# Edge-weighted mean layer of a graph network: per-step sums accumulated in PSUM instead of added by VectorE

## The reference, cut to what matters

```python
msg = h[src] * e                     # e: 100000 x 64 edge attributes
summed = segment_sum(msg, dst, 3125)
cnt = segment_sum(ones, dst, 3125)
h_total = concatenate([h, summed / maximum(cnt, 1)], axis=1)
return h_total @ W.T + b
```

## Time and profile before

| | us |
|---|---|
| Median of 3 runs | 5527.91 |
| Lowest and highest of them | 5525.43, 5542.02 |
| Span of the profiled execution, first to last instruction | 5821.8 |
| of it, the stage of the change (first attribute load to last add) | 2793.1 to 3980.2 |
| of it, the fourth layer's gathers | 4076.3 to 5382.3 |

### The profile page before, as it was taken

The page is one execution under the profiler, slowest core; times in us unless marked ns, Lnnn a source line. Parts: engine busy times, 40 slices in busy tenths (PEclk is TensorE's granted clock), DMA queues, the critical chain, the costliest instruction groups (busy, mean ns, idle before and its releaser), DMA issues. The chain is left out here.

```text
span 5821.8 us, 59032 instructions
## 1 busy us (share of the span) xinstructions
PE 3339.7 (57%) x14332; PEld 2165.0 (37%) x14332; DVE 3534.5 (61%) x6569; ACT 2187.4 (38%) x3989; POOL 2214.4 (38%) x2086
## 2 busy tenths in 40 slices
PE   5666679999999999789034332333000443433565
PEld 3555534444444444456032332333000443333452
DVE  6999989999999999310134332333211664545676
ACT  4999967878788887200000000000000111111210
POOL 0000023333333333000666777772777056666200
PEclk8999989999999999899556555555555555555556
DMA  2555544444444443787321422212111012111011
GB/s 74 163 162 162 162 131 114 119 111 111 119 109 116 116 115 97 155 187 157 57 45 38 92 47 43 50 34 22 35 28 33 9 33 36 31 36 30 5 36 35
DMA packets 546254, 474.35 MB, mean 81 GB/s; under 512 B 185774, under 2 KB 439737, under 8 KB 545086
## 3 DMA queue, kind: packets, MB, share of 16 engines
q1 hardware_dynamic: 493723, 416.13, 28.5%
q0 software_dynamic: 52288, 55.34, 5.9%
HBM read 351.39 MB, written 119.84 MB: 81 GB/s over the span
## 5 line engine op out<-in xcount | busy, mean ns | idle before, releaser
L815 PE MATMUL l_sum_ps<-arena,sums 125*65 125x500 f32 (+1 forms) x2600 | 1144.6, 578 | 9.9 <-ACT arena L776 4.8
L1740 POOL DMA_INDIRECT l_rows<-table,tile_src x782 | 768.9, 983 | 521.1 <-issue 232.6
L1143 POOL DMA_INDIRECT l_rows<-hidden_rows,tile_src x782 | 794.9, 1017 | 341.8 <-issue 231.5
L694 POOL COPY arena<-arena 125x750 f32<-125x750 f32 (+1 forms) x400 | 538.9, 1351 | 894.6 <-PE l_count_ps L804 864.9
L760 ACT ACTIVATE arena<-arena,far_left 125x750 f32<-125x750 f32 (+1 forms) x800 | 713.3, 939 | 285.7 <-DVE arena L713 285.7
L713 DVE SCALAR_TENSOR_TENSOR arena<-arena,far_past 125x750 f32<-125x750 f32 (+1 forms) x800 | 807.1, 1055 | 16.1 <-DMA arena<-score_rows 16.1
L1204 PE MATMUL l_sum_ps<-l_rows,l_hot 128*125 x1612 | 360.1, 414 | 768.6 <-issue 651.9
L724 DVE SCALAR_TENSOR_TENSOR arena<-arena,l_count_ps 125x750 f32<-125x750 f32 (+1 forms) x800 | 739.4, 970 | 100.5 <-ACT arena L765 52.0
L1934 PE MATMUL l_sum_ps<-l_rows,l_hot 128*128 x1962 | 483.6, 424 | 439.3 <-issue 268.9
L1170 DVE TENSOR_TENSOR sums<-sums,l_sum_ps 125x64 f32 x806 | 178.6, 222 | 777.9 <-DMA arena<-counts 485.6
L1204 PEld LDWEIGHTS l_sum_ps<-l_rows,l_hot 128*125 128x125 f32 x1612 | 341.3, 322 | 787.7 <-issue 786.9
(11 more groups left out here) (440 smaller groups left out, 3021.8 us busy)
## 6 DMA issues: line engine op xcount, KB each, us to landing
arena<-counts SPq DMA_DIRECT2D x300, 328.1 KB
counts<-arena SPq DMA_DIRECT2D x324, 284.4 KB
arena<-counts SPq DMA_DIRECT2D x17, 2843.8 KB
arena<-counts SPq DMA_DIRECT2D x100, 382.8 KB
l_attr<-edge_attr_in SPq DMA_DIRECT2D x97, 256.0 KB
arena<-score_rows SPq DMA_DIRECT2D x24, 732.4 KB
l_rows<-hidden_rows,tile_src POOLq DMA_INDIRECT x782
l_rows<-table,tile_src POOLq DMA_INDIRECT x782
```

Of the source, the lines that this page charges most:

```text
L694: g.tensor_copy(laid[k % 2][:, 0:n * P].rearrange("p (b v d) -> p b v d", b=n, d=D), raw[k % RAWS][:, 0:n * P].rearrange("p (v b d) -> p b ...
L815: last = nc.tensor.matmul(sum_ps[0:F + 1, c, 0:hi - lo], h_one[:, w, :], z[k % ZS][:, lo:hi], start=(w == 0), stop=(w == W - 1))
L1143: pool.indirect_dma_start(rows[:, b % RING, t, :], None, m.hidden_rows[:, :], bass.IndirectOffsetOnAxis(ap=m.tile_src[:, k:k + 1], axis=0) ...
L1740: pool.indirect_dma_start(rows[:, t % RING3, :], None, m.table3[:, :], bass.IndirectOffsetOnAxis(ap=m.tile_src[:, t:t + 1], axis=0)).then_ ...
```

## The change

The product of a step no longer goes to a fixed place and then through DVE. All 25 blocks' sums live in PSUM for the whole stage (`acc_ps`, four banks of 8 blocks of 64 columns). PE first zeroes the four banks by multiplying the identity with a zero tile, and then every step's matmul adds to its block's place, found by a register (`start=False`). DVE's `accumulate` is gone; one copy at the end moves all sums from PSUM to `m.acc`. The one-hot matrices have 8 buffers instead of 4. POOL clears a 128 x 512 zero tile instead of `m.acc`.

```diff
+HOTS = 8
+IN_ACC = 8
...
-        hot = [s.sb(f"hot{i}", [TILE, U, P]) for i in range(4)]
-        sum_ps = [s.ps(f"sum_ps{i}") for i in range(4)]
+        hot = [s.sb(f"hot{i}", [TILE, U, P]) for i in range(HOTS)]
+        zeros = s.sb("zeros", [TILE, IN_ACC * F])
+        acc_ps = s.ps("acc_ps", (128, -(-W // IN_ACC), 512))
...
-            nc.gpsimd.memset(m.acc[:, :, 0:F], 0.0).then_inc(zeroed, 1)
+            nc.gpsimd.memset(zeros[:, :], 0.0).then_inc(zeroed, 1)
...
             def one_hot(r):
-                if r >= 4:
-                    dve.wait_ge(sums_ready, r - 3)
+                if r >= HOTS:
+                    dve.wait_ge(sums_ready, r - HOTS + 1)
...
-            def accumulate(r):
-                dve.wait_ge(sums_ready, r + 1)
-                for k in steps_of(r):
-                    window = unpack.window(k)
-                    if k:
-                        dve.wait_ge(acc_ready, k)
-                    here, j = m.acc[:, bass.ds(window, 1), 0:F], k - U * r
-                    v.tensor_tensor(here, here, sum_ps[r % 4][0:P, j * F:(j + 1) * F].unsqueeze(1),
-                                    ALU.add).then_inc(acc_ready, 1)
             one_hot(0)
-            messages(0)
-            dve.wait_ge(zeroed, 1)
             for r in range(rounds_n):
...
                 if r + 1 < rounds_n:
                     one_hot(r + 1)
-                if r + 1 < batches:
-                    messages(r + 1)
-                accumulate(r)
+                if r < batches:
+                    messages(r)
+            dve.wait_ge(sums_ready, rounds_n)
+            v.tensor_copy(m.acc[:, :, 0:F], acc_ps[0:P, :, :].rearrange("p c (w f) -> p (c w) f", f=F)[:, 0:W, :])
...
+            nodes = acc_ps[0:P, :, :].rearrange("p c (w f) -> p (c w) f", f=F)
+            pe.wait_ge(zeroed, 1)
+            for c in range(-(-W // IN_ACC)):
+                nc.tensor.matmul(acc_ps[0:P, c, :], m.ident[:, 0:P], zeros[:, :], start=True, stop=True, skip_group_check=True)
             for r in range(rounds_n):
...
-                if r >= 4:
-                    pe.wait_ge(acc_ready, U * (r - 3))
...
-                    last = nc.tensor.matmul(sum_ps[r % 4][0:P, j * F:(j + 1) * F], hot[r % 4][:, j, :],
+                    last = nc.tensor.matmul(nodes[:, bass.ds(window, 1), :].rearrange("p a f -> p (a f)"), hot[r % HOTS][:, j, :],
                                             flat[:, bass.ds(place, 1), :].rearrange("p a f -> p (a f)"),
-                                            start=True, stop=True)
+                                            start=False, stop=True, skip_group_check=True)
```

More of the change, by code:

```diff
@@ L1097, in tile_sum @@
         attr = s.sb("attr", [TILE, RING, U, F])
-        hot = [s.sb(f"hot{i}", [TILE, U, P]) for i in range(4)]
-        sum_ps = [s.ps(f"sum_ps{i}") for i in range(4)]
-        hot_ready, msg_ready, sums_ready, acc_ready, zeroed = (
-            s.sem(n) for n in ("hot_ready", "msg_ready", "sums_ready", "acc_ready", "zeroed"))
+        hot = [s.sb(f"hot{i}", [TILE, U, P]) for i in range(HOTS)]
+        zeros = s.sb("zeros", [TILE, IN_ACC * F])
+        acc_ps = s.ps("acc_ps", (128, -(-W // IN_ACC), 512))
+        hot_ready, msg_ready, sums_ready, zeroed = (
+            s.sem(n) for n in ("hot_ready", "msg_ready", "sums_ready", "zeroed"))
         attr_in = s.sems("attr_in", RING)
@@ L1148, in _ @@
         def _(dve):
-            v, unpack = nc.vector, Unpack(nc, nc.vector, mybir.EngineType.DVE, m.tile_words, W)
+            v = nc.vector
             def one_hot(r):
-                if r >= 4:
-                    dve.wait_ge(sums_ready, r - 3)
-                v.tensor_tensor(hot[r % 4][:, :, :], over(m.tile_rel[:, U * r:U * r + U].unsqueeze(2), (TILE, U, P)),
+                if r >= HOTS:
+                    dve.wait_ge(sums_ready, r - HOTS + 1)
+                v.tensor_tensor(hot[r % HOTS][:, :, :], over(m.tile_rel[:, U * r:U * r + U].unsqueeze(2), (TILE, U, P)),
                                 over(m.node_row[:, :].unsqueeze(1), (TILE, U, P)), ALU.is_equal).then_inc(hot_ready, 1)
@@ L1198, in _ @@
                     pe.wait_ge(msg_ready, r + 1)
-                if r >= 4:
-                    pe.wait_ge(acc_ready, U * (r - 3))
                 flat = rows[:, :, :, :].rearrange("p b t f -> p (b t) f")
                 for k in steps_of(r):
-                    j, place = k - U * r, unpack.place(k, unpack.window(k), U * RING)
-                    last = nc.tensor.matmul(sum_ps[r % 4][0:P, j * F:(j + 1) * F], hot[r % 4][:, j, :],
+                    window = unpack.window(k)
+                    j, place = k - U * r, unpack.place(k, window, U * RING)
+                    last = nc.tensor.matmul(nodes[:, bass.ds(window, 1), :].rearrange("p a f -> p (a f)"), hot[r % HOTS][:, j, :],
                                             flat[:, bass.ds(place, 1), :].rearrange("p a f -> p (a f)"),
-                                            start=True, stop=True)
+                                            start=False, stop=True, skip_group_check=True)
                 last.then_inc(sums_ready, 1)
```

## The result

| | before | after |
|---|---|---|
| Median, same chip, 5 runs each | 5527.2 | 5507.25 |
| Lowest and highest | 5523.14, 5542.02 | 5500.64, 5515.68 |
| Time of the profiled execution itself | not recorded | 5515.68 |
| Its span | 5821.8 | 5513.9 |

The ratio is 0.9961, with a 95% interval of 0.9949 to 0.9972: 21.6 us less by the ratio, 20.0 by the medians. That is within the range given, but on the faster side of the 0.3% that a measurement of this kernel can tell. The medians that follow differ from chip to chip, so every one stands beside the kernel before on the same chip.

A forecast was written before the change was run, and what follows sets the result against it. The prediction took POOL's gathers to bound the stage. Gains of 0.9 us at the start and 1.6 at the end, 0 in the middle, made -2.5 on 5527.91, so 5525.4 us, with a range of 5410 to 5545.

The forecast's parts named there:

- A: Whole stage: POOL-bound, with few of the late-signal delays in ordinary runs; 5525 us, own range 5515 to 5545, chance 0.58.
- B: Whole stage: the late-signal delays are real and belong to the runs; 5392 to 5447 us, put at 5420, chance 0.27.
- C: Whole stage: part of the late-signal delays, as a third, is in the runs; about 5480 us, chance 0.08.
- POOL bounds the stage, DVE and PE don't.: Stage: gathers' busy time and 0.30 us gaps take 1026.4 of 1137 us; neither DVE nor PE comes near 10 us a round.
- Nothing in POOL's chain gets shorter by it ... both of those stay ... Gain 0.: Middle of the stage: removing DVE's 806 adds leaves gathers at 0.95 us, or 1.79 beside one-hot and messages; gain 0.
- 293.9 us must be the profiler's.: Profiled span 5821.8 against the runs' median 5527.91: the difference was put down to the profiler, with delays explaining 285.2 us.
- the delays: PE's signals reaching DVE and POOL late by tens of us in the profile: 110.4 + 23.0 + 151.8 = 285.2 us.
- Rival D: PE becomes the bound: some 890 us slower, 6415, chance 0.03; milder form, end only, 5538 to 5548, chance 0.04.
- Start: POOL's first instruction clears a smaller tile in 0.48 us, so gathers start earlier; gain 0.9 us (bounds 0.6 to 1.4).
- Opening matmuls: PE's four zeroing matmuls of 512 columns: 5.2 us at most, hidden under DVE's 16.51 us wait; cost 0.
- End: From the last messages to the stage's end: 19.9 us before, 18.3 after; gain 1.6, or a loss of some 10.
- Sum: All terms, start and end only: -0.9 - 1.6 = -2.5 us on the median 5527.91, giving 5525.4.

The follow-up runs named there:

- e5 to e8: Where the kernel before takes 5820.14 us: before, one-hot moved behind messages (0.9984); changed kernel, one-hot held back (1.0049), one-hots on ACT (0.9948), unchanged (0.9963).
- e8: The changed kernel, unchanged, on the chip where the kernel before takes 5820.14 us: 5791.44 us, ratio 0.9963.
- e1: The kernel before, unchanged, profiled once more: 5521.57 us against 5522.17, ratio 0.9998.
- e10: The changed kernel with its one-hot held back until PE has finished the round before, on an ordinary chip: 5545.41 us against 5524.73, ratio 1.0034.

## Why the prediction was right and where it was wrong

The measured time lies in the range by luck. The prediction's own reading, A, had 5525.4 us and a range of 5515 to 5545; 5507.25 is below it. The whole range reached down to 5410 only for B and C, which do not hold either. The 18.2 us that make up most of the gain stood in none of them.

- *POOL bounds the stage, DVE and PE don't.* Right, and more plainly than the profile of before could show: no wait but the 0.3 us.
- *"Nothing in POOL's chain gets shorter by it ... both of those stay ... Gain 0."* This is the step that failed. The gather beside one-hot and messages stays long, but in ordinary executions there were two such gathers a batch and the change leaves one. Measured: 814.0 - 795.8 = 18.2 us, where the prediction had 0. The prediction looked for a wait to go and did not ask whether the durations that it summed would stay. Its own rows 6 showed a gather at 1.79, started 0.23 us into a one-hot and over 0.82 us behind it; the count of such gathers, and where in a DVE instruction they start, was taken for fixed.
- *"293.9 us must be the profiler's."* Wrong: they are a chip's. The granted clock points the same way: 0.728 in that execution, 0.727 to 0.730 in e5 to e8, 0.738 to 0.742 in the profiles on ordinary chips. This reading was needed to see no gain, for it let the profiled execution's gathers (794.9 us, an excess of 52.0) stand for those of the runs (814.0, an excess of 71.1 in e1). In that trace the late adds let DVE fall behind, so that one-hot and messages mostly came together and met one gather, as in the earlier trace rows: the pattern that the change brings was already in the rows at hand.
- *Rival B* (delays in the runs, 5392 to 5447) did not hold: the runs shown have none. *Rival C* neither. On the chip that has the delays, the change gave 0.9963 all the same. For a profile with the delays in it the prediction allowed up to 135.9 us less, a span of 5686. The span of e8 is 5782.8, 39.0 less, and POOL still waits 82.1 us in its stage where it waited 110.4: taking the adds out of the loop does not take the delays away.
- *Rival D* did not hold. PE's round with accumulation into a place found by a register is 3.62 us, and 1612 records take 363.4 us against 359.7 in e1. Adding into PSUM costs PE at most those 3.7 us, all hidden.
- *Start.* 0.53 us for the smaller clear (0.48 estimated), against 1.43: a gain of 0.9 as forecast.
- *Opening matmuls.* 6.00 us and not at most 5.2, and hidden, as forecast.
- *End.* 19.9 us in e1 (from 3853.76 to 3873.67), 17.1 after. A gain of 2.8 against 1.6; the four rounds of PE ran together in 13.64 us, and the copy was the 1.82 estimated.
- *Sum.* 18.2 + 0.9 + 2.8 = 21.9 us, beside the 21.6 of the ratio. The prediction had the 2.5 of both ends (3.7 measured) and missed the rest. The three terms are read from one profiled execution each, of e1 and of after, and these two differ by only 8.0 us in span. From the stage's first clear to `finish_mean`'s copy (L1307) e1 takes 1081.0 us and after 1059.0, 22.0 less; but in after the stage begins 9.8 us later, and what follows it takes 4.2 us longer. Parts that the change does not touch scatter by that much, so the close match with 21.6 is partly chance.

The last of e1's adds and messages, from which its end is read:

```profile
3853.76 0.69 DVE L1160 TENSOR_TENSOR l_rows<-l_rows,l_attr 128x512 f32<-128x512 f32 x1 [4.29 <-DMA l_rows<-hidden_rows,tile_src]
...
3873.09 0.58 DVE L1170 TENSOR_TENSOR sums<-sums,l_sum_ps 125x64 f32 x2 [0.30 <-DVE sums L1170]
```

No run of its own isolates what it is in messages and one-hot that holds a gather up, their size or their inputs, but the traces hold the comparison. In the fourth layer DVE has two TENSOR_TENSOR of 64x1024 that both take 1.22 us and write to SBUF. The one into `l_spare` has both inputs in SBUF, the one into `l_z` has one of them in PSUM. The last pair has one input, in SBUF. From the timeline of after:

```profile
4060.21 1.22 DVE L1821 TENSOR_TENSOR l_spare<-values,l_first_last 64x1024 f32<-64x1024 f32 x1
4060.35 1.91 POOL L1735 DMA_INDIRECT l_rows<-table,tile_src  x1 [0.31 <-issue]
...
4149.46 1.22 DVE L1772 TENSOR_TENSOR l_z<-l_far_ps,l_spare 64x1024 f32<-64x1024 f32 x1 [61.49 <-PE l_far_ps L1893]
4150.10 0.95 POOL L1735 DMA_INDIRECT l_rows<-table,tile_src  x1 [0.30 <-issue]
...
2985.64 0.63 DVE L1350 TENSOR_SCALAR l_w_block<-l_w_block 128x896 f32<-128x896 f32 x1
2985.73 1.35 POOL L1146 DMA_INDIRECT l_rows<-hidden_rows,tile_src  x1 [0.30 <-issue]
```

The first gather starts 0.14 us into its neighbour and ends 0.83 us after it. The second has 0.58 us of its neighbour still ahead of it and takes 0.95. Over all fourteen traces 93 gathers start into the first instruction and take 0.99 to 1.99 us; 56 start into the second, and all take 0.95 or 0.96. So it is not the size, but where the inputs lie. Two inputs in SBUF are not needed, though: the TENSOR_SCALAR with one holds its gather to 1.35 us, while a TENSOR_REDUCE of 1.60 us with one, at 2991.66 in the same trace, leaves the gather at 2992.76 at 0.95. Which instructions with one input hold a gather up, and why, stays open.

## What to carry to other kernels

When one engine bounds a stage without waiting, look at the spread of its own durations before calling a change free: in the timeline, see which instruction of another engine is already running when the long ones start. Work that disturbs it is best placed together, so that one of its instructions takes the blow, or given to an engine that doesn't disturb it. When a profiled span and a median are far apart, don't explain it from one trace; the same kernel on another chip may settle it, and rows of the one are then no measure of the other.

## What was not expected of the hardware

An indirect gather of 128 rows takes POOL 0.95 us alone. One that starts while DVE runs an instruction with both inputs in SBUF (128x512 at 0.69 us, 128x1000 at 1.19 us) ends some 0.82 us after that instruction, so it takes up to 1.97 us (e10). One that starts before the DVE instruction takes 0.95. Beside adds with an input in PSUM (125x64), and beside ACT's Abs and Relu, it stays at 0.95.

One chip of those used runs this kernel in 5820 us and not in some 5525. The timeline of e8 there:

```profile
2850.35 0.65 PE L1199 MATMUL l_acc_ps<-l_rows,l_hot 128*125 x2 [2.15 <-issue]
...
2853.86 0.65 PE L1199 MATMUL l_acc_ps<-l_rows,l_hot 128*125 x2 [2.86 <-issue]
...
2919.98 0.95 POOL L1146 DMA_INDIRECT l_rows<-hidden_rows,tile_src  x1 [0.30 <-issue]
...
2922.42 0.26 PE L1199 MATMUL l_acc_ps<-l_rows,l_hot 128*125 x1 [2.54 <-issue]
...
2931.52 20.20 PE L1199 MATMUL l_acc_ps<-l_rows,l_hot 128*125 x95 [0.45 <-issue]
...
2931.88 1.79 POOL L1146 DMA_INDIRECT l_rows<-hidden_rows,tile_src  x1 [10.95 <-DMA arena<-counts]
```

PE gets through one step (x2) in 2 to 4 us, at times in 6, with nothing in the profile to wait for, until the ring is full and POOL stops at 2920.93. It stays slow for some ten more microseconds beside an idle POOL; then 95 matmuls go at full pace, 20.20 us, although POOL gathers again from 2931.88 on. So it isn't simply that POOL's work slows PE's. Why this chip does so and the others not, and whether the late signals of the earlier trace rows are the same thing, stays open.
